# Reordering the first block of each attention layer: v's projection before k's turn, and the second layer's split before the last feed-forward product

## What is computed

```python
def _layer(x, wqkv, qs, ksc, wo, lg, lb, w1, b1, w2, b2):
    h = shift_token(x)                    # second half of the channels comes from the token before
    q, k, v = jnp.split(h @ wqkv, 3, axis=-1)          # 8 heads of 64
    q = l2norm(q) * qs;  k = l2norm(k) * ksc
    q, k = rotary_xpos(q, k)
    o = local_attention(q, k, v)          # windows of 128, with the window before
    x = x + o @ wo
    h = layernorm(shift_token(x)) * lg + lb
    a, g = jnp.split(h @ w1 + b1, 2, axis=-1)
    x = x + (a * gelu(g)) @ w2 + b2
    return x
for l in range(2):
    x = _layer(x, ...)
```

## Time and profile before

| | us |
|---|---|
| median of three runs | 1553.35 |
| lowest and highest run | 1552.82, 1554.85 |
| the profiled execution's own time | 1553.17 |
| its span in the profile | 1551.4 |
| PE busy, DVE busy, ACT busy, POOL busy | 1459.8, 1160.0, 1033.3, 783.6 |

### The profile page before, as it was taken

How to read it: one execution, slowest core, us unless ns; L and a number is a source line. 1 busy time by engine, 2 the same in 40 slices (tenths; PEclk the granted TensorE clock), 3 DMA queues, 4 the chain that set the end, 5 groups by cost and what they waited for, 6 DMA issues and landing times.

```text
span 1551.4 us, 35733 instructions
## 1 busy us (share of the span) xinstructions
PE 1459.8 (94%) x10355; PEld 1210.5 (78%) x10355; DVE 1160.0 (75%) x3321; ACT 1033.3 (67%) x2612; POOL 783.6 (51%) x971
## 2 busy tenths in 40 slices
PE   7899994899999999979999979999999999799996
PEld 6458883788888888858888868888888887688885
DVE  6763686888888888885666478888888887656664
ACT  5222575788888888865454458888888888355553
POOL 4003365666666666642223546666666664334442
PEclk9999997999999999989999999999999999899998
DMA  5001234100000000002000020000000000000101
GB/s 181 1 1 46 108 97 115 53 7 5 5 5 5 5 6 6 5 6 91 8 14 7 15 65 7 6 5 5 5 5 5 5 5 8 30 28 28 54 28 55
DMA packets 57521, 44.04 MB, mean 28 GB/s; under 512 B 13214, under 2 KB 55386, under 8 KB 57442
## 3 DMA queue, kind: packets, MB, share of 16 engines
q1 hardware_dynamic: 57442, 43.07, 9.3%
HBM read 26.24 MB, written 8.39 MB: 22 GB/s over the span
## 4 chain that ended last, share of the span: by engine, by line
PE 80%; DVE 9%; ACT 4%; issue 3%; POOL 2%; DMA 1%; DVEq 0%; ACTq 0%; POOLq 0%; SPq 0%
PE bank L1987 8%; PE bank L1955 8%; PE bank L1901 7%; PE bank L1914 7%; PE bank L1820 6%; PE bank L1822 6%; PE bank L1821 6%; PE bank L1848 4%; PE bank L2058 4%; PE bank L2059 4%; PE bank L2060 4%; PE bank L1745 2%; PE bank L1746 2%; PE bank L1747 2%; PE bank L1676 2%
## 5 line engine op out<-in xcount | busy, mean ns | idle before, releaser
L1264 ACT ACTIVATE prob<-prob,neg_max 128x256 f32<-128x256 f32 x512 | 258.4, 508 | 9.2 <-DVE neg_max L2572 6.4
L826 POOL TENSOR_TENSOR rnorm<-sumsq,neg_half 128x8 f32<-128x8 f32 x128 | 212.9, 1663 | 24.5 <-POOL sumsq L823 24.5
L840 POOL TENSOR_TENSOR qk_cos<-qk_cos,qk_sin 128x512 f32<-128x512 f32 x128 | 181.2, 1416 | 60.8 <-DVE qk_cos L2436 44.8
L1820 PE MATMUL bank<-wqkv_hi,hT_hi 128*128 128x512 f32 x384 | 174.3, 454 | 17.1 <-DVE hT_lo L2422 17.1
L2058 PE MATMUL bank<-h_hi,w_hi 128*128 128x512 f32 (+1 forms) x352 | 142.3, 404 | 12.5 <-POOL h_lo L887 12.5
L1407 ACT ACTIVATE act_hi<-act_full 128x512 fp32r<-128x512 f32 x96 | 60.7, 632 | 139.2 <-DVE act_full L2761 139.2
L1822 PE MATMUL bank<-wqkv_hi,hT_lo 128*128 128x512 f32 x384 | 153.1, 399 | 0.0
L1821 PE MATMUL bank<-wqkv_lo,hT_hi 128*128 128x512 f32 x384 | 152.0, 396 | 0.0
L1955 PE MATMUL bank<-ident,prob 128*128 128x128 f32 x1024 | 147.0, 276 | 3.0 <-DVE prob L2611 2.1
L1955 PEld LDWEIGHTS bank<-ident,prob 128*128 128x128 f32 x1024 | 117.7, 140 | 30.7 <-DVE prob L2611 3.4
L2059 PE MATMUL bank<-h_hi,w_lo 128*128 128x512 f32 (+1 forms) x352 | 140.8, 400 | 0.0
(11 more groups left out here) (281 smaller groups left out, 4059.3 us busy)
## 6 DMA issues: line engine op xcount, KB each, us to landing
x_sb<-in_L_attn_hidden_states SPq DMA_DIRECT2D x8, 512.0 KB, 7.4
x_in<-in_L_attn_hidden_states SPq DMA_DIRECT2D x8, 512.0 KB, 4.9
x_scratch<-x_in SPq DMA_DIRECT2D x8, 512.0 KB, 3.1
f_x<-x_scratch SPq DMA_DIRECT2D x8, 512.0 KB, 4.5
out<-f_y SPq DMA_DIRECT2D x8, 512.0 KB, 3.1
raw<-in_L_ffn_w SPq DMA_DIRECT2D x6, 640.0 KB
hs<-x_sb SPq DMA_DIRECT2D x16, 224.0 KB
hs<-x_sb SPq DMA_DIRECT2D x64, 56.0 KB
```

Source lines behind the costliest of these rows:

```text
L826: pool.tensor_tensor(rnorm[:, part * HEADS:(part + 1) * HEADS], sumsq[:, which * HEADS:(which + 1) * HEADS], neg_half[:, 0:HEADS], ALU.pow ...
L840: pool.tensor_tensor(qk_cos[:, which], qk_cos[:, which], qk_sin[:, which], ALU.add).then_inc(z_ready[which], 1)
L1264: act.activation(prob[:, h], prob[:, h], ACT.Exp, bias=neg_max[:, h:h + 1], scale=-1.0, accum_out=psums[:, h:h + 1]).then_inc(exped, 1)
L1820: pe.matmul(bank[:, to], hT_hi[:, c], wqkv_hi[:, c, cols], start=(c == 0), stop=False)
```

## The change

It touches block 0 of both layers and nothing in the loops.

1. PE, block 0 of both layers: v is projected before k is turned, where before k was turned first.
2. PE, second layer: block 0's transposes stand ahead of the product of chunk 4; the product of chunk 5 stands behind block 0's k and q projections and ahead of v's. The wait for the last share of `wqkv_lo` moves from ahead of k's projection to ahead of v's.
3. ACT, in group 7 of the first layer: `hT_hi` of the second layer's block 0 (`next_hi`) stands between `gelu_sb` and `act_hi` of chunk 5.
4. DVE, in the same group: `hT_lo` (`next_lo`) stands between `act_full` and `act_lo` of chunk 5; `add_up` of group 7 stands behind the whole of `step(0)`.

No instruction is added or removed.

```diff
 ACT
-                    if not lay and type(b) is int and b == 0:
+                    if not ahead and type(b) is int and b == 0:
                         return
...
+                def next_hi():
+
+                    act.wait_ge(hT_ps, k0 + NB + 1)
+                    act.wait_ge(v_raw, k0 + NB)
+                    act.activation(hT_hi[:], bank[:, 3, 0:2 * P].rearrange("p (c t) -> p c t", c=DC), ACT.Copy).then_inc(hT_hi_ready, 1)
...
                         act.activation(gelu_sb[0:w, j % 2], bank[0:w, j % 2], ACT.Gelu, bias=b1_sb[0:w, 1, j:j + 1]).then_inc(g_ready, 1)
+                        if j == FC - 1 and lay + 1 < DEPTH and type(g) is int and g == NG - 1:
+                            next_hi()
                         act.wait_ge(act_ready, FC * k + j + 1)
 PE
-                    if live(n, 0):
+                    if type(n) is int and n == 0:
+                        if lay:
+                            down(lay * NG - 1, FC - 1)
+                        pe.wait_ge(ffn_split, FIRST + SPLITS * lay)
+                        project(n, 2, v_raw)
+                        turn_qk(n, 1)
+                    elif live(n, 0):
                         turn_qk(n, 1)
                         project(n, 2, v_raw)
 
                 if lay:
+                    pe.wait_ge(act_ready, FC * (lay * NG - 1) + FC - 2)
+                    transposes(0, ahead=True)
                     down(lay * NG - 1, FC - 2)
-                    pe.wait_ge(act_ready, FC * (lay * NG - 1) + FC - 1)
-                    transposes(0, ahead=True)
-                    down(lay * NG - 1, FC - 1)
                     pe.wait_ge(act_ready, FC * lay * NG)
-                pe.wait_ge(ffn_split, FIRST + SPLITS * lay)
+                pe.wait_ge(ffn_split, FIRST + SPLITS * lay - (1 if lay else 0))
 DVE
-                lo(0, ahead=True)
-                if lay:
-                    add_up(lay * NG - 1, NG - 1)
-                else:
+                if not lay:
+                    lo(0, ahead=True)
                     dve.wait_ge(x_made, NB)
                     dve.wait_ge(x1_stored, 16 * NG)
                 dve.wait_ge(sc_made, MADE + TABLES * (lay + 1))
                 for n in range(6):
                     step(n, n % 2)
+                    if lay and n == 0:
+                        add_up(lay * NG - 1, NG - 1)
...
+                def next_lo():
+
+                    dve.wait_ge(hT_hi_ready, k0 + NB + 1)
+                    dve.wait_ge(v_raw, k0 + NB)
+                    dve.tensor_tensor(hT_lo[:], bank[:, 3, 0:2 * P].rearrange("p (c t) -> p c t", c=DC), hT_hi[:], ALU.subtract).then_inc(hT_lo_ready, 1)
...
+                        if j == FC - 1 and not last and type(g) is int and g == NG - 1:
+                            next_lo()
```

More of the change, by code:

```diff
@@ L1158, in _, with hi @@
                 k0 = lay * NB
-                def hi(b):
-                    if not lay and type(b) is int and b == 0:
+                def hi(b, ahead=False):
+                    if not ahead and type(b) is int and b == 0:
                         return
```

## The result

The changed kernel took 1549.76 us (median of eight runs, 1548.07 to 1550.39), the kernel before 1553.96 us in its eight runs beside them (1552.73 to 1554.95). The ratio is 0.9971, with a 95% interval from 0.9960 to 0.9982. In another set of runs (after_again) it gave 0.9972 (0.9962 to 0.9982). So the change makes the kernel 0.3% faster, by 4.2 us of the medians. The profiled execution took 1549.94 us, 3.2 us less than the one shown of before.

The account below looks back on a forecast made before the run. PE was taken to bound the kernel, busy 1459.8 us. Gains of 0.9 us in the first layer and 2.9 in the second, 3.8 together, off the profiled 1553.17 gave 1549.4 us; range 1546.0 to 1551.3.

Parts of the forecast that it names:

- the low clock in both layers: Likeliest case: block 1's k runs at half clock behind the wait in each layer; 1549.4 us, chance 0.52.
- The waits: PE's idle time ahead of block 0's k turn: from 5.21 to about 3.6 us, and from 5.39 to about 2.2.
- The first layer's gain: v ahead of k's turn in block 0: 0.9 us taken, from 0.2 (scores also slow) to 1.1.
- my 271.66: Start of block 1's k in the first layer, with turns and transposes at half clock; 273.91 before.
- The second layer's gain: Chunk 5's product behind q, v ahead of k's turn: 2.9 us taken, between 2.3 and 3.2.
- The covers: Where the layers meet: `h_in`, split, later `act_hi`, last `wqkv_lo` share cost nothing; moved `add_up` free at half clock.
- the loops pass the gain on: If PE reaches a loop some microseconds earlier, all that follows is that much earlier.
- Only the moved product counts: Rival: v's move gives nothing, chunk 5's product in the second layer gives 1.6 us; 1551.6 us, chance 0.11.
- Slower: Rival: clock stays half until block 2's scores in each layer, 5.7 us slower; 1558.9 us, chance 0.05.
- The clock holds: Rival: full clock through the shortened waits; one layer 1547.8 or 1547.0 us, chance 0.26; both 1545.4, chance 0.06.

Follow-up runs that it names:

- add_up_early: The changed kernel with DVE's `add_up` of group 7 back ahead of `step(0)`, behind the split; 1.0010 of the kernel before.
- after_filled: The changed kernel plus 15 and 9 products nobody reads ahead of k's turn in block 0 of the first and second layer; 0.9957 of the kernel before.
- v_first_only: The kernel before with only v projected ahead of k's turn in block 0 of both layers, the layers' meeting unchanged; 0.9983 of the kernel before.
- filled_twice: The changed kernel plus unread products ahead of block 0's k turn (15 and 9) and block 0's second scores (6 in block 1); 0.9941 of the kernel before.

## Why the prediction was right

The forecast was 1549.4 us and the measured time 1549.76; the case was the one that I held likeliest, the low clock in both layers. That the two times are 0.4 us apart is partly luck. The forecast started from an execution of 1553.17 us, while the kernel before had a median of 1553.96 beside the changed one; of the gain itself I forecast 3.8 us, and the medians give 4.2, the profiles 3.2. By its own steps:

**The waits.** Forecast 3.6 and 2.2 us, measured 3.67 and 2.22. k's turn in the first layer stayed where it was, and v went into the wait at full clock. In the first layer two small errors cancel: v's six products, straight behind q, fill 1.39 us and not 1.60, and q ended 0.15 us later after block 0's k than before.

**The first layer's gain.** Forecast 0.9 us (0.2 to 1.1), measured 0.94 at the mask, counted from the layer's k. The clock fell behind k's turn, not before it, which made the start of block 1's k 0.37 earlier than my 271.66; the scores at half clock then held the mask, as I had feared for the low end. The reason that I gave for taking 0.9, near the upper end, did not hold: I expected the clock back some 3.7 us into the unbroken stretch from block 1's k on, and it came back at 276.2, 4.9 us into it and behind the scores. The two errors cancel, so the hit on 0.9 is luck; the range of 0.2 to 1.1 was sound.

**The second layer's gain.** Forecast 2.9 us, measured 1.7 for chunk 5's product (4.76 to 3.06) and 1.4 from k to block 2's k, 3.1 in all. For chunk 5's product I had 1.6, and for v's place the rest, 1.3. From the transposes to chunk 4's product it is only 0.13 us, not the 0.31 that they took in the earlier trace rows on the way to chunk 5's narrower product; chunk 4's own product took 0.08 more.

**The covers.** `h_in`, the split (0.38 us to spare, forecast 0.42), the later `act_hi` and the last share of `wqkv_lo` cost nothing. `add_up` fitted without a gap, and block 1's k followed its transposes as soon as in the first layer (1.57 and 1.56 us). add_up_early shows what its place is worth, 3.5 us in the chain, and after_filled that it becomes the bound once the clock holds.

**What I had no term for.** I took it that the loops pass the gain on. They do, but the feed-forward phases begin with waits as well, and the clock came back from these at its own time. The stretches of the first `up` products at half clock, of before and then of after:

```profile
694.30:698.90 4.60, 4.60 (x11) 3.63 (x12) 3.81 (x3) 0.69 (x1) 2.28 (x1) 0.50 0.00 0
...
1331.80:1337.20 5.40, 5.40 (x13) 4.24 (x14) 3.79 (x3) 0.69 (x1) 2.25 (x1) 0.50 0.03 7
```

```profile
693.60:699.30 5.70, 5.70 (x14) 4.45 (x15) 4.04 (x4) 0.69 (x1) 2.25 (x1) 0.50 0.02 3
...
1328.40:1334.20 5.80, 5.80 (x14) 4.56 (x15) 4.12 (x4) 0.69 (x1) 2.26 (x1) 0.50 0.07 15
```

In the first layer `up` begins at 694.25 before and at 693.51 after, and the clock is back near 699.0 before and 699.4 after: 4.8 us of `up` at half clock became 5.9. In the second layer (from 1331.73 and 1328.34) 5.6 us became 5.95. Half of the difference, 0.6 and 0.2 us, is the most that this can cost. The first `up` and DVE's first `act_full` of the first layer, before:

```profile
694.25 0.80 PE L2058 MATMUL bank<-h_hi,w_hi 128*128 128x512 f32 x1 [6.25 <-POOL h_lo L887]
...
699.50 0.75 DVE L2761 SCALAR_TENSOR_TENSOR act_full<-bank,b_sb,gelu_sb 128x512 f32<-128x512 f32 x1 [1.24 <-PE bank L2060]
```

That is 5.25 us, and 5.53 in the changed kernel: 0.3 us lost. In the second layer it is 5.53 in both. Counted from block 0's k in the first layer, the gain was 0.84 at the end of that layer's attention and 0.57 at group 7's product of chunk 3, and 3.5 at the end of the second layer's attention and 3.3 at the end of the span: 0.3 and 0.2 lost. The profile of after_again agrees (1.0 at the end of the first layer's attention, 3.3 at that of the second, 3.2 at the end of the span). Three profiled executions are all that this rests on; whether it is so on the mean of many, no run here shows, and in other runs this term was a gain. The medians, 4.2 us apart, sit above the 3.2 of the profiles, and this remains unexplained.

**The rivals.** "Only the moved product counts" falls with v_first_only, which gains by v's move alone. "Slower" falls with the windows: the clock is back at 276.2 and 911.0, before block 1's v (281.19 and 916.28). In v_first_only's second layer it came back only at 914.7, still before v. "The clock holds" didn't happen in the two profiled executions of the changed kernel. I had priced it at 4 us (7.8 less 3.8). after_filled has 3.8 of that at the masks but loses most of it again in block 1, a step that I hadn't foreseen; filled_twice has 3.7 at block 2's k. That it comes out 5.2 us faster by the medians is due in part to the feed-forward phases.

## What to carry to other kernels

Ahead of a chain that another engine works through, look for any work of the waiting engine that doesn't depend on it and move it in front; but subtract what the moved work did where it stood, here to bring the clock back. After such a move, ask for each later stretch at what clock it will run, and price it by rows at both levels: 1.60 or 2.85 us for the same six products. Before a difference of 1 us between two traces is put down to an edit, look whether half-clock stretches elsewhere have moved: here the starts of the feed-forward phases took 0.6 us or gave 1.0 by themselves. An edit that reorders one engine can hang on a second on another: chunk 5's product behind the projections was a gain only with `add_up` behind `step(0)`.

## What the runs showed of the hardware that I had not expected

- The granted clock can fall behind waits through which it had stayed at 2.4 GHz in another run of nearly the same work: before kept 1.00 through block 1's waits of 1.87 and 0.69 us, after_filled fell to 0.50 behind waits of 1.83 and 0.71 us. A wait that "keeps the clock" in one trace is no promise.
- Adding 104 products to PE's idle time, in a kernel that PE bounds, made it 7 us faster.
- 3.8 us of f32 transposes alone kept the clock at 1.00, as products did.
- Half clock behind nearly the same wait doesn't always last equally long: around k's turn the clock stood at 0.50 for at least 6.7 us in both layers of the changed kernel, but for at least 10.1 us in the second layer of v_first_only.
